# One maximum instruction over two PSUM banks, and two score banks instead of three, in an attention chain on one Trainium2 core

## The reference

```python
scores = einsum('bqhd,bkhd->bhqk', q, k) / sqrt(8)
attn   = softmax(scores, axis=-1)                 # over 1601 context keys, or over 256 own keys
out    = einsum('bhqk,bkhd->bqhd', attn, v)
x      = x + (out @ Wp + bp)                      # with a gate in the two self attentions
```

## Time and profile before

| | us |
|---|---|
| median of 3 runs | 6772.17 |
| lowest and highest | 6766.07 and 6781.2 |
| the profiled execution, its own time | 6777.38 |
| span in the profile, first to last instruction | 6775.6 |
| mean granted TensorE clock | 0.963 |

### The profile page before, as it was taken

How to read it: one execution, slowest core, us unless ns; L and a number is a source line. 1 busy time by engine, 2 the same in 40 slices (tenths; PEclk the granted TensorE clock), 3 DMA queues, 4 the chain that set the end, 5 groups by cost and what they waited for, 6 DMA issues and landing times.

```text
span 6775.6 us, 156710 instructions
## 1 busy us (share of the span) xinstructions
PE 6148.7 (91%) x49714; PEld 3142.0 (46%) x49714; DVE 4444.0 (66%) x9848; ACT 4234.5 (62%) x8158; POOL 982.1 (14%) x1660
## 2 busy tenths in 40 slices
PE   6999999999777999999998777799999999979998
PEld 3444444444444444444443344344444444435554
DVE  5777777776555777777775355577777777724333
ACT  3777777777665777777775465566766767642223
POOL 3112112211111111111110011221211211100000
PEclk9999999999998999999999899899999999989998
DMA  2222222221112222222220111222212222101110
GB/s 84 74 71 60 62 76 66 55 73 43 56 56 73 77 66 65 67 73 76 66 64 20 37 56 61 67 56 75 66 52 77 56 63 67 46 32 41 42 42 24
DMA packets 181002, 403.68 MB, mean 60 GB/s; under 512 B 16992, under 2 KB 124560, under 8 KB 166416
## 3 DMA queue, kind: packets, MB, share of 16 engines
q1 hardware_dynamic: 180752, 400.01, 22.0%
HBM read 316.81 MB, written 83.14 MB: 59 GB/s over the span
## 4 chain that ended last, share of the span: by engine, by line
PE 76%; DVE 8%; ACT 6%; issue 6%; DMA 3%; SPq 1%; POOL 1%; DVEq 0%; ACTq 0%; POOLq 0%
PE bank L1112 19%; PE bank L1084 17%; PE bank L1067 16%; DVE MX L1409 3%; DMA QP<-scr_q 3%; PE bank L653 2%; PE bank L1038 2%; PE bank L1033 2%; PE bank L644 2%; PE bank L1099 2%; PE bank L670 1%; PE bank L1088 1%; ACT P L1242 1%; PE bank L582 1%; PE bank L1048 1%
## 5 line engine op out<-in xcount | busy, mean ns | idle before, releaser
L1242 ACT ACTIVATE P<-bank 128x512 f32<-128x512 f32 (+1 forms) x5504 | 3078.5, 596 | 1483.5 <-PE bank L1067 1457.9
L1409 DVE TENSOR_REDUCE MX<-bank 128x1 f32<-128x400 f32 (+1 forms) x6144 | 3214.4, 569 | 1129.9 <-PE bank L1084 1046.9
L1067 PE MATMUL bank<-QP,KP 128*128 128x256 bf16 (+1 forms) x11008 | 2091.0, 277 | 104.2 <-ACT QP L1253 42.9
L1084 PE MATMUL bank<-KP,QP 96*128 96x400 bf16 (+1 forms) x6144 | 2099.1, 342 | 67.6 <-DMA QP<-scr_q 46.7
L1112 PE MATMUL bank<-P,VA 128*25 128x256 f32 (+1 forms) x22016 | 1776.8, 395 | 20.2 <-issue 9.6
L1067 PEld LDWEIGHTS bank<-QP,KP 128*128 128x128 bf16 (+1 forms) x11008 | 1030.2, 101 | 791.0 <-issue 180.0
L1084 PEld LDWEIGHTS bank<-KP,QP 96*128 96x128 bf16 x6144 | 594.2, 97 | 1015.6 <-DVE MX L1409 598.5
L1112 PEld LDWEIGHTS bank<-P,VA 128*25 128x25 f32 (+1 forms) x22016 | 403.8, 102 | 741.7 <-issue 623.8
L1412 DVE TENSOR_REDUCE MX<-bank 128x2 f32<-128x512 f32 x512 | 327.0, 685 | 304.5 <-PE bank L1088 304.4
L1532 POOL COPY VA<-VN 128x416 f32<-128x416 f32 (+1 forms) x320 | 138.9, 434 | 2569.5 <-PE bank L1112 1290.5
L1253 ACT CAST QP<-bank 2x512 bf16<-2x512 f32 x640 | 338.8, 575 | 133.6 <-PE bank L1099 127.6
(11 more groups left out here) (209 smaller groups left out, 4705.5 us busy)
## 6 DMA issues: line engine op xcount, KB each, us to landing
KP<-scr_k SPq DMA_DIRECT2D x192, 900.6 KB
QP<-scr_q SPq DMA_DIRECT2D x960, 48.0 KB
CN<-ctx_n SPq DMA_DIRECT2D x40, 768.0 KB
scr_k<-KSF SPq DMA_DIRECT2D x48, 600.8 KB, 3.3
scr_k<-KSF SPq DMA_DIRECT2D x48, 600.0 KB, 3.4
CT<-ctx_t SPq DMA_DIRECT2D x24, 800.5 KB, 4.4
KP<-scr_ks SPq DMA_DIRECT2D x128, 144.0 KB
scr_q<-QS SPq DMA_DIRECT2D x80, 192.0 KB, 2.1
```

Source lines behind the costliest of these rows:

```text
L1067: last = nc.tensor.matmul(SC[ph.score_bank(2 * (g * ph.nt + t) + half)][0:kt, k * N:(k + 1) * N], KP[g][:, c0:c0 + kt], QP[g][:, h * N:(h ...
L1084: last = nc.tensor.matmul(dst[:, 0:n], QP[g][0:MR, h * N + qt * 128:h * N + qt * 128 + 128], KP[g][0:MR, h * ph.nk + c0:h * ph.nk + c0 + n ...
L1242: nc.scalar.activation(P[v % 2][0:kt, half * 2 * N:(half + 1) * 2 * N], SC[ph.score_bank(2 * (g * ph.nt + t) + half)][0:kt, :], ACT.Exp, s ...
L1409: nc.vector.tensor_reduce(MX[:, r, c:c + 1], src[:, 0:CHUNKS[c][1]], AX.X, ALU.max).then_inc(sem("max_done"), 1)
```

## The change

The 32 maximum matmuls of a group become 16 pairs. A pair writes the two halves of a two-bank PSUM tensor `MP` (there are two such tensors, four banks), and one DVE instruction of 2x401 columns reduces both halves into two columns of `MX`. The chunks become four windows of 401 keys that overlap by one column. A pair waits for the reduction two pairs before. The pairs are spread over slots 0 to 10 as before: two in slots 0, 2, 4, 6, 8 and one in 1, 3, 5, 7, 9, 10. A slot's first pair stands after its first scores and its second pair after its second scores; none stands after the values. In a self stage the four double matmuls become two pairs, each reduced by one instruction of 4x256 columns. The banks for this come from the scores, which now have two: `SC[half]`, and each half waits for the exponential of the half two before. The rows of `shift_rows` go to the two halves of `MP[1]`, and pair 1 waits for both row copies. Stage l3 keeps its single banks, under other names.

```diff
+SPANS = [(0, 401), (400, 401), (800, 401), (1200, 401)]
...
-        self.nm = 2 * G * len(CHUNKS) if self.cross else G
+        self.nm = G * len(SPANS) if self.cross else G // 2
...
-        SC, MB, OB, MISC = bank[0:3], bank[3:6], bank[6], bank[7]
+        SC = [ctx.enter_context(nc.psum_tensor("bank%d" % k, [128, 512], f32)) for k in range(2)]
+        MP = [ctx.enter_context(nc.psum_tensor("pair%d" % k, [128, 1024], f32)) for k in range(2)]
...
             def scores(ph, b, g, t, half):
-                u = 2 * (g * ph.nt + t) + half
-                pe.wait_ge(sem("probs_full"), at("probs_full", b, ph.score_before(u) + 1))
+                pe.wait_ge(sem("probs_full"), at("probs_full", b, 2 * (g * ph.nt + t) + half - 1))
...
             def maximum(ph, b, g, j):          # PE
-                elif j < 3:
-                    wait(pe, "rows_done", at("rows_done", b, 2 * g + j - 2))
-                if j >= len(MB):
-                    pe.wait_ge(sem("max_done"), at("max_done", b, g * ph.nm + j - len(MB) + 1))
+                elif j == 1:
+                    wait(pe, "rows_done", at("rows_done", b, 2 * g))
+                if j >= 2:
+                    pe.wait_ge(sem("max_done"), at("max_done", b, g * ph.nm + j - 1))
+                for k in range(2):
+                    if ph.cross:
+                        h, qt, (c0, n) = j // 4, j // 2 % 2, SPANS[j % 2 * 2 + k]
+                        last = nc.tensor.matmul(MP[j % 2][:, k * 512:k * 512 + n],
+                                                QP[g][0:MR, h * N + qt * 128:h * N + qt * 128 + 128],
+                                                KP[g][0:MR, h * ph.nk + c0:h * ph.nk + c0 + n], start=True, stop=True)
...
             def maximum(ph, b, g, j):          # DVE
-                    r, c = j // len(CHUNKS), j % len(CHUNKS)
-                    nc.vector.tensor_reduce(MX[:, r, c:c + 1], src[:, 0:CHUNKS[c][1]], AX.X, ALU.max).then_inc(
-                        sem("max_done"), 1)
+                    r, c = j // 2, j % 2 * 2
+                    nc.vector.tensor_reduce(MX[:, r, c:c + 2],
+                                            MP[j % 2][:, :].rearrange("p (t k) -> p t k", t=2)[:, :, 0:SPANS[0][1]],
+                                            AX.X, ALU.max).then_inc(sem("max_done"), 1)
```

More of the change, by code:

```diff
@@ L144, in maximum_at @@
         return [j for j in range(self.nm) if min(j * spread // self.nm, n - 1) == t]
[L146 to L156, removed]
     def prep_slots(self, host):
@@ L1066, in scores @@
                     c0 = h * ph.nk + t * 128
-                    last = nc.tensor.matmul(SC[ph.score_bank(2 * (g * ph.nt + t) + half)][0:kt, k * N:(k + 1) * N], KP[g][:, c0:c0 + kt],
+                    last = nc.tensor.matmul(SC[half][0:kt, k * N:(k + 1) * N], KP[g][:, c0:c0 + kt],
                                             QP[g][:, h * N:(h + 1) * N], start=True, stop=True)
@@ L1075, in maximum @@
                     pe.wait_ge(sem("packed_loaded%d" % g), at("packed_loaded%d" % g, b, 64))
-                elif j < 3:
-                    wait(pe, "rows_done", at("rows_done", b, 2 * g + j - 2))
-                if j >= len(MB):
-                    pe.wait_ge(sem("max_done"), at("max_done", b, g * ph.nm + j - len(MB) + 1))
-                dst = MB[j % len(MB)]
-                if ph.cross:
-                    r, c = j // len(CHUNKS), j % len(CHUNKS)
[L1083 to L1090, removed]
+                elif j == 1:
[8 more added lines that the diff above has]
+                                                KP[g][0:MR, h * ph.nk + c0:h * ph.nk + c0 + n], start=True, stop=True)
+                    else:
+                        h = 2 * j + k
+                        for qt in range(2):
+                            last = nc.tensor.matmul(MP[j % 2][:, (2 * k + qt) * N:(2 * k + qt + 1) * N],
+                                                    QP[g][0:MR, h * N + qt * 128:h * N + qt * 128 + 128],
+                                                    KP[g][0:MR, h * ph.nk:(h + 1) * ph.nk], start=True, stop=True)
                 last.then_inc(sem("max_full"), 1)
@@ L1096, in shift_rows @@
                 for half in range(2):
-                    dst = MB[1 + half]
                     for r in range(4):
-                        last = nc.tensor.matmul(dst[MR:MR + 2, r * 128:(r + 1) * 128], NMB[g % 2][:, 4 * half + r, :],
+                        c = half * 512 + r * 128
+                        last = nc.tensor.matmul(MP[1][MR:MR + 2, c:c + 128], NMB[g % 2][:, 4 * half + r, :],
                                                 IDB[:, :], start=True, stop=True)
```

13 lines of the change are left out of this document (7 added, 6 removed).

## The result

| | us |
|---|---|
| before, median (4 runs beside the changed kernel) | 6776.68 |
| after, median of 4 runs | 6734.4 (6733.67 to 6735.17) |
| after / before | 0.9939, 95% interval 0.9922 to 0.9956 |
| after, the profiled execution | 6733.98, span 6732.2, mean clock 0.967 |

The change made the kernel 0.6% faster. The forecast was 6794, slower. The time lies inside the wide range (6650 to 6850) and outside the forecast's own (6755 to 6830); the sign is wrong, and so is the likeliest case.

A forecast was written before the change was run, and what follows sets the result against it. PE's order was taken as the bound in most slots, with DVE nearly full. Terms -95 - 10 + 2 + 49 + 5 - 1 + 72 = +22 on 6777.4, less 5.2, gave 6794 us; own range 6755 to 6830, wide range 6650 to 6850.

The forecast's parts named there:

- the likeliest case: The forecast's own case for the whole kernel: 6794 us, range 6755 to 6830, chance 0.55.
- (f): PE code place at loop edges: c1 gets c2's nine-block edge, +72 us; a0 still fits, c2 keeps nine blocks.
- the code lies better: Rival on PE code place: c1 still fits, 6722 us (chance 0.20), or c2 fits as well, 6645 (0.12).
- (a): DVE's wide reduction: 0.90 us a pair instead of 0.96, 0.07 less, bounds 0.84 to 0.96.
- two banks cost two: Rival on DVE's wide instruction: it gains nothing, only the `q` wait goes, 6841 us, chance 0.13.
- (b): PE's waits for DVE in cross stages: -2.3 us an element in a0 and c2, -1.4 in c1, -95 in all.
- (c): PE's order of maximum matmuls, none behind the values: -10 us (0 to -20), with +2 for extra columns.
- (d): Two score banks: first scores of groups 1 and 2 wait for late exponentials, +1.03 us an element, +49 in all.
- (e): Self stages: the chain to `shift_rows` gets about 0.05 us longer in 128 groups, +5 us (-15 to +20).

The follow-up runs named there:

- b_fit: The kernel before with 174 more PE instructions (satisfied waits) ahead of c2's first maximum, so c2's loop body fits eight blocks: 6709.0 us, ratio 0.9918.
- a_fit: The changed kernel with 90 more PE instructions (satisfied waits) ahead of c1's first maximum, so c1 and c2 fit eight blocks: 6653.5 us, ratio 0.9834.
- a_fit_split: The changed kernel with c1 and c2 inside eight blocks, each pair reduced by two 401-column instructions instead of one of 802: 6673.9 us, ratio 0.9855.

## Why the prediction was wrong

The step that failed stands in part (f): "c2 starts 128 earlier, at o + 206: nine as before", from which c2's edge was to cost what it had. Nine blocks are what it fetches. But its tail went from o + 29 to o + 91, and from there the branch takes 0.35 us for 3.6, and the half clock behind the stop is gone too. I had one price for nine blocks and no thought of where in the ninth the body ends. That is 76 us: c2's fifteen periods fell by 94.4, of which b_fit shows 76 to be the edge. With it the sum had been 6794 - 76 = 6718, 16 below the 6734 measured.

I had written down this number's neighbour: the rival "the code lies better" priced c2's edge at 77. But its mechanism was a body that fits, with no fetch, and its margin (o above 61) is not what happened. Its 6722 is near the measured 6734 by luck: it has c1 resident and c2 as slow as before, and it was c1 that became slow and c2 that was freed. The Trainium skill ("Runtime: NRT & Kernel Launch", Instruction fetch mechanics) has a taken branch to a block not held stall for the fetch. c1's edge agrees; c2's (nine packets, no stop) shows that the fetch can come before the branch.

The other steps, against the two kernels on good places and the traces:

- (f) for c1: +72 forecast; its periods are 1473.4 against a_fit's 1403.5, +70. The size is partly luck. It was c2's stop and half clock taken over; c1 had a shorter stop (1.8 us for 3.6) and in eight of thirteen elements the second one, of which the prediction had nothing. That a0 stays resident: right.
- (a) 0.90 a pair: 0.965 in a row, 0.99 alone. The bound 0.96 ("two banks cost two") was nearer, in a row; the 0.07 saved is what a pair that stands alone has. That rival's 6841 is out all the same: with two instructions a pair (a_fit_split) the changed kernel is still 35 us faster than b_fit.
- (b) and (c): -2.3 an element in a0 and c2; group 0 without its last slot fell by 2.05 in a0 and 2.3 in c2. In c1 it fell by 1.9 for 1.4. The `q` wait went, 39.1 us of idle time on `ON` to none. `shift_rows` still waits 1.10, as forecast.
- (d) +1.03 an element: +1.18, +1.18 and +1.00 in the last slots of groups 0 and 1 of a0, c1 and c2. In place it was right; alone only +31 us remain of +49.
- (e) +5: s1 and s2 together -7.5. The periods got shorter, not longer; no run tells why.
- All of it but (f): -50 forecast, -55 measured (6709.0 to 6653.5).
- Not foreseen: single stops in the code that runs once. PE's idle time of 5.5 us in a0's last element is gone, in s2's it is 3.5 and 6.1 for 6.0, and the stretch in m2 and l3 is 8.5 longer, with a granted clock of 0.82 for 0.93 in some 70 us of it. No run was made on these.

## What to carry to other kernels

When an edit changes how many instructions a loop body has, or what stands ahead of it, compute where every large body begins and ends in its blocks before pricing anything else; here the place was worth 70 us in one stage and 76 in another, and the edit itself 55. Compare two versions only on places that are alike, and try an edit of a few already satisfied waits first: here it won 81 us where the change had won 42. A gain that comes with a wide instruction may be the order that came with it, so try the order alone.

## What the runs showed of the hardware

- A PE loop body that touches nine 16 KB blocks fetches all nine an iteration, one that fits into eight fetches none. The stop at the branch runs from 3.6 us to none, by how far the body reaches into the ninth. Near the border (o + 91) the same branch showed both outcomes within one execution.
- The stop at the branch can have a second one behind it, at the next border. After branches of 1.78 to 1.85 us c1's elements took 94.5 and 95.1 us without it, at a granted clock of 1.00, and 100.4 to 101.5 with it (3.8 to 4.1 us), at 0.97 to 0.98. Look for both, and for the clock behind them.
- The view of idle times can name the wrong releaser for such a stop (ACT, in c1), where the earlier trace rows had "issue".
- One reduction over two PSUM banks takes 0.99 us; two single ones side by side take 1.06. Sixteen in a row took 15.47 us, 32 single ones 15.49 on three banks and 16.05 on the banks of the pairs.
- Two row copies (2x512) take 1.06 us on ACT and 1.31 on DVE; where DVE was idle (group 1), the kernel with its copy was the faster one all the same.
